# The places of three weight splits in the queues of VectorE and ScalarE, in a transformer block with a mixture of experts

## The chip, the cores and the metric

The kernel runs on one core of a Trainium2 chip, in float32 from HBM to HBM. The engines of the core are TensorE (PE, with its weight loads apart as PEld), VectorE (DVE), ScalarE (ACT), GpSimd (POOL) and SyncE (SP, which issues DMAs here). They work each through a queue of its own in order, and wait for each other by semaphores. The metric is the time of one execution in microseconds of the device. Three runs of the kernel before are there, and one profiled execution, from which all rows come. The granted clock of TensorE stands at one of its two levels, 1.2 or 2.4 GHz; its mean over the profiled execution was 0.864 of full speed.

## What is computed

The input is x, 32 sequences of 64 tokens with 256 features. Four layers follow one another:

```python
# 1: adapter: one of 16 domain experts for each sequence, then a layer norm
hidden = gelu(x @ down_W.T + down_b)
hidden = where(valid, hidden @ expert_W[idx].T + expert_b[idx], hidden) + domain_emb[idx]
x = layernorm(hidden @ up_W.T + up_b + x) * gamma + beta
# 2: attention with 16 heads of 16, a bias for each pair, a mask; feed-forward 256 -> 1024 -> 256
x = ln(x) * (1 + scale) + shift
probs = softmax(where(mask, -inf, q @ k.T / 4 + bias))
x = x + (probs @ v) @ Wo + bo
h = ln(x) * g2 + beta2
x = x + gelu2(h @ W1 + b1) @ W2 + b2
# 3: pairs of features rotated by theta and phi of the sequence
x = stack([x0*ct + x1*st, -x0*st + x1*ct, x2*cp + x3*sp, -x2*sp + x3*cp])
# 4: norm, norm over time, style, then a mixture of 8 experts, the best 2 for each token
h = ((ln(x)*g + b) normed over the tokens) * gamma3 + beta3
probs = softmax(h @ router)
y = sum over the best two experts e of gate_e * (relu(h @ w1[e] + b1[e]) @ w2[e] + b2[e])
return x + y
```

The expert weights of layer 4 (8 experts, two matrices of 256 x 1024 each) come as float32. The kernel multiplies the tokens with them as pairs of float16 halves: a high half, and the low half that the high one leaves over.

## The kernel before

**Stages.** The tokens are worked in NCH = 4 chunks of 512 (8 sequences). After a setup, chunk 0's layer 1 and 2 run; then a loop over c = 0, 1, 2 ("round c") holds on every engine, interleaved by hand, the second half of chunk c (feed-forward, rotation, norms, routing) with the attention of chunk c + 1 and the adapter of chunks c + 2 and c + 3. A tail ends the last chunk, a plan sorts the tokens by expert, and the experts' phase goes over 39 tiles of 128 rows from about 490 us to the end.

**Splits.** Beside all this, the expert weights are turned into halves and stored in HBM (`w_split`), to be loaded again for the experts' phase. There are 16 parts of 1 MB, numbered (c, q): chunk c = 0 to 3 carries parts q = 0 to 3, the two matrices of experts 2c and 2c + 1. All of them go through one tile `stage` and one tile `split`, so one part follows another:

- SP, `load_part(c, q)` (L430) waits until the low split of the part before is done, then issues the load into `stage`. `store_part(c, q)` (L437) waits for the low split of its part and issues the store from `split`. SP's queue holds store(c, q), then load(c, q + 1), and among them the loads of the attention's bias and of x.
- ACT, `split_high(c, q)` (L652): waits for the load and for the store of the part before, then writes the high half (L657).
- DVE, `split_low(c, q)` (L916): waits for the high half, then writes the low half (L920) and so frees `stage`.

**Order in a round.** It is written out by hand, in the loops at L779 (ACT), L1275 (DVE) and L1668 (PE). What stands where in round c matters:

- ACT: `feed_forward_in(c)` copies the transposed norm of PE to `h_f` (L707), `feed_forward(c, ...)` does the eight gelus (L713), split_high(c + 1, 0), exponentials, split_high(c + 1, 1), exponentials, queries and keys, `context`, `norm3(c)` (the copy L719), `context`, split_high(c + 1, 2), `token_gates`, `rows` (L731), and last `store(c)`, which waits for DVE's `accumulate` and issues the DMA of the chunk's output (L743). In rounds 1 and 2, split_high(c, 3) stands behind the fifth of the eight gelus; so it does for the last chunk, behind the loop.
- DVE: `values`, the adapter's residual and `norms` of chunk c + 2, split_low(c, 3) in rounds 1 and 2, `scores(0)` (additions L1033, maximum L1035), `scale_norm`, split_low(c + 1, 0), `scores(1)`, `sums(0)` (L1040, L1041), `rotate` (L1066 to L1078), `sums(1)`, `norm3` (statistics L953 to L948, and L963, which releases PE's transposes), split_low(c + 1, 1), `style` (L1091 to L1108), `residual`, the choice of experts, `fill_rows` (L1166), `norm2` of chunk c + 1 (the lines of norm3 again), `accumulate` (L1180), the adapter's `hidden` (L974), split_low(c + 1, 2).
- PE: `turn2(c)` (L1424), feed-forward (L1562, L1571) around the scores of chunk c + 1 (L1498), queries and keys (L1459), `context(c + 1, 0)` (L1516, L1526), `turn3(c)` (L1424), `context(c + 1, 1)`, output projection (L1542), routing, and the start of chunk c + 3.
- POOL: `residual`, mask of the biases (L517), the maxima subtracted (L536), the probabilities (L542), the odd half of the rotation (L560 to L563), and `dispatch(c)`, eight indirect DMAs (L573) that write the rows of the chunk to the place of their experts.

`split_low` in full, since it is what moves:

```python
def split_low(c, q):
    dve.wait_ge(split_hi.sem, split_hi.of(c, q + 1))
    part, high, low = split_of(q)
    dve.scalar_tensor_tensor(low, part, W_SCALE, high, ALU.mult, ALU.subtract).then_inc(split_lo.sem, 1)
```

## Time and profile before

| What | us |
|---|---|
| three runs: lowest, median, highest | 752.83, 753.59, 755.81 |
| the profiled execution: its own time | 752.83 |
| the profiled execution: span from first to last instruction | 751.0 |
| busy in the span: PE, DVE, ACT, POOL | 576.8, 484.2, 262.0, 271.4 |
| PE busy in round 0 (137 to 230), round 1 (230 to 330), round 2 (330 to 417) | 80.94, 77.45, 67.97 |
| DVE busy in the same stretches | 81.05, 78.51, 60.99 |
| start of PE's feed-forward (L1562) of chunks 1, 2 and 3 | 224.48, 324.86, 411.36 |
| end of the last weight store, and of the loads of the first five experts' weights | 431.85, 473.39 |

Busy time alone tells little here, since in the rounds neither PE nor DVE is busy throughout. The questions are which engine waits for which, and what stands in the queue behind a waiting instruction. The profile has four views for this. The chain of waits is followed back from the last instruction, at each step to what released it. The timeline of an engine gives each instruction with the idle time in front of it and what ended that. The groups of one tile gather all that reads or writes it. The DMA issues carry the time from issue to landing.

### The profile page before, as it was taken

To read this page: it belongs to the slowest core of one execution; us is meant where nothing else is said; L and a number is where in the kernel's file an instruction comes from. 1 tells how busy PE (TensorE), PEld (TensorE's weight loads), DVE (VectorE), ACT (ScalarE), POOL (GpSimd) and SP (SyncE) were. 2 spreads that over 40 slices of the span, in tenths; PEclk is the share of its full clock that TensorE was granted. 3 is DMA by queue.
4 is the path that set the end of the run, shared out by engine and by line. 5 is a ranking of instruction groups with operands and counts; after the bars stand their busy time and mean duration, and the time that the engine had idled before them with its cause. 6 is when DMAs were issued, how large, how long until landed. Compare 5 with 4: busy or idle time off the path is not lost.

```text
span 751.0 us, 16208 instructions
## 1 busy us (share of the span) xinstructions
PE 576.8 (77%) x5068; PEld 432.0 (58%) x5069; DVE 484.2 (64%) x1306; ACT 262.0 (35%) x548; POOL 271.4 (36%) x200
## 2 busy tenths in 40 slices
PE   3518587996979877769576963439999999999992
PEld 1416384583864756638474452327778777777771
DVE  5673785899789798626987136715656565656661
ACT  1215534425343253143332301004444444443440
POOL 0731728167055370327803220400323333323332
PEclk9559699999888999779885895559999999999997
DMA  8622473130325323174132567465222222222320
GB/s 287 231 81 78 147 254 140 36 114 0 113 99 211 134 92 113 44 266 166 59 113 78 175 238 261 181 242 168 48 43 47 42 43 39 42 45 34 49 42 1
DMA packets 41144, 86.28 MB, mean 115 GB/s; under 512 B 7317, under 2 KB 31790, under 8 KB 37006
## 3 DMA queue, kind: packets, MB, share of 16 engines
q1 hardware_dynamic: 22896, 65.13, 24.9%
q0 software_dynamic: 7200, 8.60, 6.7%
q10 hardware_dynamic: 11006, 12.01, 5.2%
q8 instruction: 25, 0.41, 0.2%
q14 instruction: 17, 0.14, 0.1%
HBM read 57.18 MB, written 29.44 MB: 115 GB/s over the span
## 4 chain that ended last, share of the span: by engine, by line
PE 49%; DVE 22%; issue 9%; DMA 7%; ACT 4%; ACTq 3%; POOL 3%; another core or an unknown queue 1%; POOLq 0%; SPq 0%; DVEq 0%
PE bank L1740 7%; PE bank L1562 6%; PE bank L1729 4%; PE bank L1731 4%; PE bank L1730 4%; DMA out_x<-x_kept,ids 4%; PE bank L1571 4%; PE bank L1741 3%; PE bank L1459 2%; DMA stage<-in_moe_w 2%; PE bank L1526 2%; PE bank L1542 2%; DVE stats L953 2%; PE bank L1516 2%; DVE w_moe L1076 2%
## 5 line engine op out<-in xcount | busy, mean ns | idle before, releaser
L1729 PE MATMUL bank<-xs_f,w_moe 128*128 128x128 f16 x624 | 123.9, 221 | 7.2 <-issue 5.7
L1731 PE MATMUL bank<-xs_f,w_moe 128*128 128x128 f16 x624 | 123.9, 221 | 0.0
L1730 PE MATMUL bank<-xs_f,w_moe 128*128 128x128 f16 x624 | 123.4, 221 | 0.0
L831 ACT ACTIVATE stage<-bank,cols 128x128 f32<-128x128 f32 x312 | 88.6, 376 | 95.6 <-PE bank L1731 82.9
L1729 PEld LDWEIGHTS bank<-xs_f,w_moe 128*128 x624 | 61.4, 98 | 43.1 <-issue 14.4
L629 POOL DMA_INDIRECT out_x<-x_kept,ids x39 | 62.0, 1590 | 64.4 <-DVE x_kept L1379 34.4
L1740 PE MATMUL bank<-w_moe,split 128*128 x208 | 78.6, 380 | 0.9
L573 POOL DMA_INDIRECT dispatched<-disp,slot x32 | 34.6, 1080 | 119.4 <-DVE disp L1166 55.6
L1562 PE MATMUL bank<-w_moe 128*128 128x512 f32 x128 | 63.0, 655 | 9.9 <-ACT w_moe L707 9.9
L1730 PEld LDWEIGHTS bank<-xs_f,w_moe 128*128 x624 | 61.6, 99 | 2.6
L920 DVE SCALAR_TENSOR_TENSOR split<-stage,split 128x2048 f16<-128x2048 f32 x16 | 39.9, 2494 | 35.2 <-ACT split L657 35.2
L1731 PEld LDWEIGHTS bank<-xs_f,w_moe 128*128 x624 | 61.4, 98 | 0.9
L1571 PE MATMUL bank<-w,w_moe 128*128 128x256 f32 x256 | 58.3, 387 | 0.8 <-ACT w_moe L713 0.8
L1741 PE MATMUL bank<-w_moe,split 128*128 x208 | 56.7, 273 | 0.0
L625 POOL COPY ids<-meta 128x1 uint32 (+1 forms) x39 | 13.2, 339 | 117.4 <-DMA out_x<-x_kept,ids 100.8
L657 ACT ACTIVATE split<-stage 128x2048 f16<-128x2048 f32 x16 | 30.5, 1906 | 69.9 <-DMA stage<-in_moe_w 53.4
L1571 PEld LDWEIGHTS bank<-w,w_moe 128*128 128x128 f32 x256 | 49.1, 194 | 9.0 <-ACT w_moe L713 1.6
L536 POOL TENSOR_TENSOR w_moe<-w_moe,sc_max 128x2048 f32<-128x2048 f32 x8 | 30.9, 3868 | 62.0 <-DVE sc_max L1035 62.0
L1424 PE MATMUL bank<-mats,w_moe 128*128 128x128 f32 x96 | 17.7, 345 | 45.8 <-DVE w_moe L963 45.6
L1562 PEld LDWEIGHTS bank<-w_moe 128*128 128x128 f32 x128 | 26.7, 212 | 44.2 <-issue 31.8
L517 POOL TENSOR_TENSOR w_moe<-w_moe,mask_add 128x512 f32<-128x512 f32 x32 | 41.5, 1334 | 21.6 <-DMA w_moe<-in_bias 21.5
L1364 DVE COPY xs_f<-bank 128x512 f16<-128x512 f16 x40 | 16.9, 424 | 48.1 <-PE bank L1719 48.1
(242 smaller groups left out, 1248.1 us busy)
## 6 DMA issues: line engine op xcount, KB each, us to landing
stage<-in_moe_w SPq DMA_DIRECT2D x16, 1024.0 KB, 8.4
w_split<-split SPq DMA_DIRECT2D x16, 1024.0 KB, 4.9
w_moe<-w_split SPq DMA_DIRECT2D x8, 2048.0 KB, 8.1
w_moe<-in_bias SPq DMA_DIRECT2D x8, 1024.0 KB, 10.5
xs<-dispatched ACTq DMA_DIRECT2D x41, 130.0 KB
w_moe<-in_x_f SPq DMA_DIRECT2D x4, 512.0 KB, 5.8
w_moe<-in_x_t SPq DMA_DIRECT2D x4, 512.0 KB, 5.0
out_x<-x4b ACTq DMA_DIRECT2D x4, 512.0 KB
```

The costliest lines, as they stand in the source:

```text
L517: pool.tensor_tensor(sc[u][:, r], sc[u][:, r], mask_add[:, bass.ds(c * TT + 2 * u, 2), :].unsqueeze(2).broadcast_to([P, 2, 4, S]), ALU.add ...
L573: pool.indirect_dma_start(out=xs_dram[:, :], out_offset=bass.IndirectOffsetOnAxis(ap=slot[:, a, i:i + 1], axis=0), in_=disp[:, i, :], in_o ...
L629: pool.indirect_dma_start(out=out[:, :], out_offset=bass.IndirectOffsetOnAxis(ap=ids[j][:, 0:1], axis=0), in_=ys[j], in_offset=None, bound ...
L831: ins = act.activation(h32[j][:, f, :], bank[2 * j + g][:, P * (f % 4):P * (f % 4) + P], ACT.Relu, bias=moe_b1[:, bass.ds(e, 1), f], scale ...
L920: dve.scalar_tensor_tensor(low, part, W_SCALE, high, ALU.mult, ALU.subtract).then_inc(split_lo.sem, 1)
L1562: mm = pe.matmul(bank[4 + f % 2][:], w1[:, k, P * f:P * f + P], h_f[:, k, :], start=(k == 0), stop=(k == KD - 1))
L1571: mm = pe.matmul(bank[6 + i // 2][:, D * (i % 2):D * (i % 2) + D], ff[:, f, P * i:P * i + P], w2[:, f, :], start=(f == 0), stop=(f == KF - 1))
L1729: pe.matmul(o, hi, xs_f[j][:, k, :], start=(k == 0), stop=False)
L1730: pe.matmul(o, hi, xs_f[j][:, KD + k, :], start=False, stop=False)
L1731: mm = pe.matmul(o, lo, xs_f[j][:, k, :], start=False, stop=(k == KD - 1))
L1740: pe.matmul(o, h_hi[m][:, f, :], rows_of, start=(f == 0), stop=(f == KF - 1), skip_group_check=True)
L1741: mm = pe.matmul(o[:, 0:D], h_lo[m][:, f, :], rows_of[:, 0:D], start=False, stop=(f == KF - 1), skip_group_check=True)
```

## The change

The splits of parts 1, 2 and 3 of a chunk move to other places in the queues of DVE and ACT. On DVE, split_low(c + 1, 1) stands in front of `norm3` instead of behind it; split_low(c + 1, 2) stands in front of `norm2` instead of at the end of the round; split_low(c + 1, 3) stands at the end of round c, instead of in front of `scores(0)` of the next round (for the last chunk: it stays in front of the tail). On ACT, split_high(c + 1, 3) stands in front of `store(c)` instead of between the gelus of the next round's feed-forward. The code of SP, PE and POOL is untouched; SP's waits for the splits are met at other times. No instruction is added or taken away, and the same values are computed.

```diff
@@ ACT, loop over the rounds
             for c in range(NCH - 1):
                 feed_forward_in(c)
-                if c > 0:
-                    feed_forward(c, range(5))
-                    split_high(c, 3)
-                    feed_forward(c, range(5, KF))
-                else:
-                    feed_forward(c, range(KF))
+                feed_forward(c, range(KF))
                 split_high(c + 1, 0)
...
                     keep(c + 2)
                     values(c + 2)
+                split_high(c + 1, 3)
                 store(c)
             feed_forward_in(NCH - 1)
-            feed_forward(NCH - 1, range(5))
-            split_high(NCH - 1, 3)
-            feed_forward(NCH - 1, range(5, KF))
+            feed_forward(NCH - 1, range(KF))
@@ DVE, loop over the rounds
                     norms()
-                if c > 0:
-                    split_low(c, 3)
                 scores(0)
...
                 sums(1)
+                split_low(c + 1, 1)
                 norm3()
-                split_low(c + 1, 1)
                 style()
...
                 fill_rows()
+                split_low(c + 1, 2)
                 norm2()
                 accumulate()
                 if c + 3 < NCH:
                     hidden, adapter_residual, norms = adapter(c + 3)
                     hidden()
-                split_low(c + 1, 2)
-            split_low(NCH - 1, 3)
+                split_low(c + 1, 3)
```

ACT's queue at the end of round 2 and the feed-forward of the last chunk; L657 is the high split, L743 the issue of the output's DMA, L707 the copy, L713 the gelus:

```order
 L731 ACTIVATE disp<-bank 128x2x256 x2
+L657 ACTIVATE split<-stage 128x8x256
 L743 DMA out_x<-x4b 128x4x256
 L707 ACTIVATE w_moe<-bank,cols 128x512 x2
 L713 ACT_TABLE_LOAD
-L713 ACTIVATE w_moe<-bank,cols 128x512 x5
-L657 ACTIVATE split<-stage 128x8x256
-L713 ACTIVATE w_moe<-bank,cols 128x512 x3
+L713 ACTIVATE w_moe<-bank,cols 128x512 x8
```

The high split of part 3 has moved from between the gelus to a place in front of the output's DMA and of the copy.

DVE's queue at the end of round 2, before; L1166 is `fill_rows`, L953 to L963 `norm2`, L1180 `accumulate`, L920 the low split:

```order
L1166 TENSOR_TENSOR disp<-bank,disp 128x2x256 x2
L953 BN_STATS stats<-w_moe 128x6 x4
...
L963 TENSOR_SCALAR w_moe<-w_moe,mv,rstd 128x256 x4
L1180 TENSOR_TENSOR x4b<-bank,w_moe 128x512 x2
L920 SCALAR_TENSOR_TENSOR split<-stage,split 128x2048
L920 SCALAR_TENSOR_TENSOR split<-stage,split 128x8x256
L1066 TENSOR_TENSOR w_moe<-bank,w_moe 128x512 x2
```

The same place in the changed kernel, where the lines of these functions are six lower (the low split is L914):

```order
L1160 TENSOR_TENSOR disp<-bank,disp 128x2x256 x2
L914 SCALAR_TENSOR_TENSOR split<-stage,split 128x2048
L947 BN_STATS stats<-w_moe 128x6 x4
...
L957 TENSOR_SCALAR w_moe<-w_moe,mv,rstd 128x256 x4
L1174 TENSOR_TENSOR x4b<-bank,w_moe 128x512 x2
L914 SCALAR_TENSOR_TENSOR split<-stage,split 128x8x256
L1060 TENSOR_TENSOR w_moe<-bank,w_moe 128x512 x2
```

The low split of part 2 now stands in front of the statistics of norm2; that of part 3 keeps its place in front of the last chunk's rotation, but its wait is for a high split that stands elsewhere on ACT.

DVE's queue around norm3 of round 2, before; L1040 and L1041 are `sums(1)`, L953 to L963 norm3, L1091 the start of `style`:

```order
L1040 TENSOR_REDUCE sc_sum<-w_moe 128x32
L1041 RECIPROCAL sc_inv<-sc_sum 128x32
L953 BN_STATS stats<-w_moe 128x6 x4
...
L963 TENSOR_SCALAR w_moe<-w_moe,mv,rstd 128x256 x4
L920 SCALAR_TENSOR_TENSOR split<-stage,split 128x8x256
L1091 BN_STATS stats<-h 128x6 x16
```

And in the changed kernel:

```order
L1034 TENSOR_REDUCE sc_sum<-w_moe 128x32
L1035 RECIPROCAL sc_inv<-sc_sum 128x32
L914 SCALAR_TENSOR_TENSOR split<-stage,split 128x8x256
L947 BN_STATS stats<-w_moe 128x6 x4
...
L957 TENSOR_SCALAR w_moe<-w_moe,mv,rstd 128x256 x4
L1085 BN_STATS stats<-h 128x6 x16
```

The low split of part 1 has moved from between norm3 and `style` to a place between the sums and norm3.

## Rows read from the trace of the kernel before

**Rows 1.** Chain of waits, whole program: start us, us, what stood in it.
```profile
248.46 8.43 DMA stage<-in_moe_w
256.91 1.92 ACT split L657
...
340.86 8.30 DMA stage<-in_moe_w
...
398.94 10.49 issue
409.43 0.38 ACTq L743
409.86 1.46 ACT w_moe L707 x2
```

**Rows 2.** Tile `stage`: durations ns min/median/max, first and last start; last its loads.
```profile
L657 ACT ACTIVATE split<-stage x16: 1893/1910/1911, 40.5 to 423.7; 128x2048 f16<-128x2048 f32 x16
L920 DVE SCALAR_TENSOR_TENSOR split<-stage,split x16: 2228/2284/4733, 51.0 to 425.7; 128x2048 f16<-128x2048 f32 x16
...
DMA to landing us min/median/max: 5.8/8.4/9.4
```

**Rows 3.** Timeline of DVE: start us, us, engine, line, what [idle before <-releaser].
```profile
258.85 2.29 DVE L920 SCALAR_TENSOR_TENSOR split<-stage,split 128x2048 f16<-128x2048 f32 x1 [4.89 <-ACT split L657]
...
351.12 2.31 DVE L920 SCALAR_TENSOR_TENSOR split<-stage,split 128x2048 f16<-128x2048 f32 x1 [4.56 <-ACT split L657]
```

**Rows 4.** Timelines of DVE, POOL and PE around norm3 of round 0, same columns.
```profile
178.49 1.34 DVE L953 BATCH_NORM_STATS2 stats<-w_moe 128x6 f32<-128x256 f32 x4
...
187.75 2.28 DVE L920 SCALAR_TENSOR_TENSOR split<-stage,split 128x2048 f16<-128x2048 f32 x1
189.96 2.11 DVE L1091 BATCH_NORM_STATS2 stats<-h 128x6 f32<-128x64 f32 x16
...
178.65 3.62 POOL L542 TENSOR_TENSOR w_moe<-w_moe,sc_inv 128x2048 f32<-128x2048 f32 x1 [1.64 <-DVE sc_inv L1041]
...
187.89 1.97 PE L1424 MATMUL bank<-mats,w_moe 128*128 128x128 f32 x8 [5.87 <-DVE w_moe L963]
```

**Rows 5.** Timelines of DVE and POOL where a split meets POOL, early chunks.
```profile
92.06 2.23 DVE L920 SCALAR_TENSOR_TENSOR split<-stage,split 128x2048 f16<-128x2048 f32 x1
...
155.69 4.73 DVE L920 SCALAR_TENSOR_TENSOR split<-stage,split 128x2048 f16<-128x2048 f32 x1
...
92.22 5.54 POOL L542 TENSOR_TENSOR w_moe<-w_moe,sc_inv 128x2048 f32<-128x2048 f32 x1 [0.42 <-DVE sc_inv L1041]
```

**Rows 6.** Timelines of DVE and SP at the end of round 2.
```profile
401.79 1.27 DVE L1166 TENSOR_TENSOR disp<-bank,disp 128x512 f16<-128x512 f32 x2
...
409.32 2.27 DVE L920 SCALAR_TENSOR_TENSOR split<-stage,split 128x2048 f16<-128x2048 f32 x1
...
412.01 0.43 SPq L433 DMA_DIRECT2D stage<-in_moe_w  x1
```

**Rows 7.** Timelines of DVE, ACT and PE at the ends of rounds 0 and 1.
```profile
210.25 1.27 DVE L1166 TENSOR_TENSOR disp<-bank,disp 128x512 f16<-128x512 f32 x2
...
307.85 1.27 DVE L1166 TENSOR_TENSOR disp<-bank,disp 128x512 f16<-128x512 f32 x2
...
321.60 1.29 DVE L1180 TENSOR_TENSOR x4b<-bank,w_moe 128x512 f32<-128x512 f32 x2 [7.34 <-remote]
...
221.62 1.51 ACT L707 ACTIVATE w_moe<-bank,cols 128x512 f32<-128x512 f32 x2 [8.49 <-remote]
...
224.48 16.40 PE L1562 MATMUL bank<-w_moe 128*128 128x512 f32 x32
```

**Rows 8.** Timelines of PE, DVE and POOL in round 2.
```profile
350.27 2.66 PE L1498 MATMUL bank<-w_moe 32*64 32x128 f32 x64
...
353.36 2.47 DVE L1033 TENSOR_TENSOR w_moe<-bank,w_moe 128x512 f32<-128x512 f32 x4
...
361.81 3.62 POOL L542 TENSOR_TENSOR w_moe<-w_moe,sc_inv 128x2048 f32<-128x2048 f32 x1
```

## The prediction

> **What bounds the kernel now.** I read the chain of waits first, then the groups of the tile `stage`, then the timelines of DVE, ACT, PE, POOL and of SP's DMA issues around each place where a split stands. "Round c" is one pass of the loop over c = 0, 1, 2 (about 137 to 230, 230 to 330 and 330 to 417 us); "split(c, q)" is part q of chunk c, with its high half on ACT (L657) and its low half on DVE (L920).
>
> The chain of the first 500 us runs over all engines in turn, with no engine that bounds it alone. Two of its pieces are waits for a part of the expert weights: in rounds 1 and 2 the load of part (c+1, 0) and the high split behind it stand in the chain with 8.43 + 1.92 us and again with 8.30 us. At the end of round 2 it waits on ACT, whose next work, the copy that feeds feed-forward of the last chunk, starts at 409.86 [rows 1]. A low split costs DVE 2.28 us in the median, a high split costs ACT 1.91, and a load lands 8.4 us after its issue, 5.8 at best and 9.4 at worst [rows 2]. What the two waits of the chain cost is less than 10 us each, because other work goes on below them: DVE idled 4.89 and 4.56 us in front of the low split (c+1, 0) [rows 3]. These two are what the change can win; 9.5 us is the most.
>
> **Part 1: split (c+1, 1) in front of norm3, three times.** Before, this split stood behind norm3 and was free. In round 0 norm3 released the transposes on PE at 187.89, after PE had idled 5.87 us for them; `style` on DVE could not start before ACT had copied their result, and began at 189.96. The split filled just this gap, 187.75 to 190.03 [rows 4]. In front of norm3 it delays norm3, the transposes, the context products and output projection queued behind them on PE, and `style`, and the gap behind norm3 stays open. Cost 2.2 us in each of three rounds, since the row of the statistics at 178.49 follows the softmax sums without idle time. Bounds: 0, if norm3 had to wait for POOL's half of the rotation anyway, and the stretched form below.
>
> Here DVE and POOL also meet. The rows show that a low split and a tensor operation of POOL exclude one another: with the split first, POOL's multiplication took 5.54 us where it takes 3.62; with POOL first, the split took 4.73 where it takes 2.28 [rows 4, 5]. In the new place POOL's multiplication by the inverse sums is released by the same DVE instruction that the split follows; in the pattern of 92.06 the split started first, by 0.16 us, so I take 2.2 for DVE and shift POOL. The small operations of norm3 wait for POOL then as they do now, only later.
>
> The Trainium skill, SBUF — State Buffer, section "SBUF: two separate sides", says that VectorE and GpSimd share one port pair under an exclusive lock, which the instruction that starts first keeps to its end; the trace agrees (5.54 and 4.73). What follows if POOL comes first is rival 2.
>
> **Part 2: split (c+1, 2) in front of norm2, and split (c+1, 3) at the end of the round.** The load of part 3 is issued only when the low split of part 2 is done, since both use the one `stage` tile. On ACT the high split of part 3 now stands in front of `store` and of the copy that feeds feed-forward. ACT works in order, so feed-forward of the next chunk waits for: low split 2, issue, load, high split, issue of the store. Before, none of these stood there.
>
> End of round 2, first with no shift from earlier. `fill_rows` ends at 401.79 + 1.27 = 403.06 [rows 6]. Low split 2.28: 405.34. From a low split's end (409.32 + 2.27 = 411.59) to the issue of the load at 412.01 it takes 0.42 [rows 6]: 405.76. Load 8.4: 414.16. High split 1.91 and 0.02 to start it: 416.09. The store's issue, by the gap from 409.43 to 409.86 [rows 1], 0.43: 416.52. The copy started at 409.86, so this boundary costs **6.7 us**. The 2.28 us for norm2 and the accumulation lie inside it: they would end near 411.6. PE's feed-forward, queued behind the copy, moves by the same 6.7. The landing sets the bounds: 5.8 gives 4.1, 9.4 gives 7.7.
>
> By the Trainium skill, DMA: Bandwidth & Descriptors, section "Anatomy of one DMA — SWDGE (gpsimd) path", a transfer costs about 2.0 us and its bytes over 436 GB/s; for 1 MiB that is an estimate of 4.4 us, with which the boundary would cost 2.7. The rows of this kernel, with 1 MB out and 1 MB in queued together, show 8.4, and they decide.
>
> End of round 0, shifted by 2.2 from part 1: `fill_rows` ended at 210.25 + 1.27 = 211.52 [rows 7]. 211.52 + 2.2 + 2.28 + 0.42 + 8.4 + 1.93 + 0.43 = 227.2 for a copy that started at 221.62: 5.6 us later. PE's feed-forward began at 224.48, behind another wait, and the copy takes 1.5, so it begins near 228.7, 4.2 later. DVE has its own split(1, 3) near 226.8 to 229.0 and is some 6 us late for the norms of chunk 3.
>
> End of round 1: `fill_rows` ended at 307.85 + 1.27 = 309.12, and with the shift of 0.8 derived below the high split would be done near 323.0. Before, DVE stood still for 7.34 us until 321.60 in front of the accumulation, a wait whose cause the profile doesn't name (PE's result came late) [rows 7]; the copy came behind it. If this wait is still there, the splits hide in it, and the boundary costs only what it is shifted, 0.8.
>
> **Part 3: what comes back.** In round 1 the delay of 4 to 6 us meets the wait that is gone. Split(1, 3) no longer stands in front of the scores (2.2 us), load (2, 0) is long landed (4.89 us of idling gone), and the masks of POOL, whose bias load no longer stands behind a late weight load, slow fewer of DVE's norms (about 3 us). But DVE is then next held by POOL (low split (2, 0) behind the subtraction of the maxima, as in the row of 4.73) and by PE, which is 3 us late with its scores. My estimate from these pieces is that the second maximum of the scores comes 1.4 us early. Part 1 takes 2.2 again: round 1 hands on +0.8.
>
> In round 2 PE's last scores were done at 350.27 + 2.66 = 352.93, while DVE's additions ran to 353.36 + 2.47 = 355.83, late by the wait for split (3, 0). Without it they end 0.7 behind PE: 352.93 + 0.8 + 0.7 = 354.4, 1.4 early; the POOL multiplication at 361.81, which holds up the rotation, moves with them [rows 8]. With part 1's 2.2: +0.8 at `fill_rows`. So of the 9.5 us nearly all goes to repay the boundaries and part 1, and the last boundary, behind which no weight wait is left to remove, is paid in full.
>
> **Sum.** 0.8 + 6.7 = 7.5 us. Nothing behind it gives this back: the weights were loaded long before the experts began, and the experts' phase shifts as a whole. The profiled execution took 752.83 us (its span 751.0), so 752.83 + 7.5 = 760.3; it is the fastest of the three runs, whose median is 753.59, and against that the sum is 761.1. I give **761.0**.
>
> **Rivals.**
> Rival 1, the delays add up: the norms of chunk 3 gain nothing from the earlier masks (3 us), and rounds 1 and 2 hand on +3.7 instead of +0.8. Then 753.6 + 3.7 + 6.7 = 764.0. For it: the DVE and POOL rows depend on which comes first by tenths of a microsecond. Against: round 2 has slack of its own on PE.
> Rival 2, POOL first at the lock in front of norm3: the split takes up to 2.28 + 3.62, of which 1.8 comes back because norm3's first small operation no longer waits; some 1.8 more per round, and not all of it survives to the end: about 763.
> Rival 3, a shorter load: at the last boundary the queue is emptier, the load lands in 5.8 us, or the rounds before gain 3 us more: 761.1 - 2.6 to 761.1 - 5.6, about 757.
> Rival 4, not slower: the ends of the rounds hide their loads and the removed waits count in full: 753.6 - 4.89 - 4.56 + 3 x 2.2 = 750.7. For it: DVE's 7.34 us at the end of round 1 show that such a hole exists. Against: at the end of round 2 there is none; it decides from the point at which the load needs under 8.4 - 6.7 = 1.7 us there, or round 2 reaches `fill_rows` 6.7 us early, and no row shows a load under 5.8.
> Rival 5, the change does nothing, since the order of two queues is unlike what I read: 753.6. The listings of the new order speak against it.
>
> **How the numbers follow.** Forecast 0.57, rival 1 0.17, rival 2 0.10, rival 3 0.10, rival 4 0.04, rival 5 0.02. Range: 756.5 to 765.0 holds the forecast with both bounds of the load (758.5 to 762.1), rivals 1 and 2 and most of rival 3. A change of 0.5%, 3.8 us, is about what can be told from none. Under 749.8 lies a part of rival 4, 0.02; within 749.8 to 757.4 the rest of it, rival 5 and about half of rival 3, 0.10; above, 0.88.
>
> **What would show it.** Right: in the last round ACT idles some 7 us before the high split that stands in front of the store, for the load, and the copy L707 starts near 417 instead of 409.86; DVE no longer idles 4.9 and 4.6 us before split (c+1, 0); DVE has an idle gap of about 2 us behind norm3, waiting for L719; the high split of part 3 of round 1 hardly moves the copy. Wrong: a load in the last round that landed before accumulation, or a start of the statistics of norm3 in round 2 that is over 3 us early or late.

## The result, and the profile after

The changed kernel takes 760.9 us in the median of five runs (759.66 to 762.53) beside 753.44 for the kernel before on the same chip: a ratio of 1.0097 (95% interval 1.0083 to 1.0112). The forecast was 761.0. In a second run of its own the change stood at 1.0103 (1.0075 to 1.0131; last experiment). The profiled execution of after took 761.58 us, its span is 759.8 against 751.0.

Line numbers of after are lower than those of before: DVE's by 6 (the split is L914), PE's by 8 (the transposes are L1416, the feed-forward L1554); those of ACT, POOL and SP are the same.

The tile `stage`, as in [rows 2], first. The columns are shortest, median and longest duration in ns, then first and last start:

```profile
L657 ACT ACTIVATE split<-stage x16: 1893/1909/1912, 40.4 to 416.9; 128x2048 f16<-128x2048 f32 x16
L914 DVE SCALAR_TENSOR_TENSOR split<-stage,split x16: 2228/2282/4736, 51.1 to 418.9; 128x2048 f16<-128x2048 f32 x16
```

The same work takes the same time; what changed is who waits. The chain of waits of after (start, length, what) has lost both loads of a part (c + 1, 0) that [rows 1] showed, and has three others, one at the end of each round:

```profile
215.63 9.41 DMA stage<-in_moe_w
...
312.91 9.44 DMA stage<-in_moe_w
...
407.64 9.25 DMA stage<-in_moe_w
```

The last of them in full, from the timelines of DVE, SP, ACT and PE in after (start, duration, what, and in brackets the idle time in front with its releaser):

```profile
403.77 1.27 DVE L1160 TENSOR_TENSOR disp<-bank,disp 128x512 f16<-128x512 f32 x2
404.96 2.27 DVE L914 SCALAR_TENSOR_TENSOR split<-stage,split 128x2048 f16<-128x2048 f32 x1
407.64 0.43 SPq L433 DMA_DIRECT2D stage<-in_moe_w  x1
412.27 1.28 DVE L1174 TENSOR_TENSOR x4b<-bank,w_moe 128x512 f32<-128x512 f32 x2
416.92 1.91 ACT L657 ACTIVATE split<-stage 128x2048 f16<-128x2048 f32 x1 [15.99 <-DMA stage<-in_moe_w]
416.92 0.38 ACTq L743 DMA_DIRECT2D out_x<-x4b  x1
418.73 1.43 ACT L707 ACTIVATE w_moe<-bank,cols 128x512 f32<-128x512 f32 x2
420.22 2.08 PE L1554 MATMUL bank<-w_moe 128*128 128x512 f32 x2 [5.84 <-ACT w_moe L707]
```

DVE's accumulation ends at 413.55, so the store and the copy L707 could go then. They go at 416.92 and 418.73, because the high split stands ahead of them on ACT and its load landed 9.25 us after the issue. Against [rows 6] and [rows 1], `fill_rows` is 1.98 us late (403.77 for 401.79) and the copy 8.87 (418.73 for 409.86): this one boundary makes 6.9 us.

The place of norm3 in round 0, answering [rows 4], on DVE, POOL and PE of after:

```profile
177.61 2.23 DVE L914 SCALAR_TENSOR_TENSOR split<-stage,split 128x2048 f16<-128x2048 f32 x1
177.77 5.53 POOL L542 TENSOR_TENSOR w_moe<-w_moe,sc_inv 128x2048 f32<-128x2048 f32 x1 [1.66 <-DVE sc_inv L1035]
188.93 1.97 PE L1416 MATMUL bank<-mats,w_moe 128*128 128x128 f32 x8 [7.80 <-DVE w_moe L957]
190.89 2.12 DVE L1085 BATCH_NORM_STATS2 stats<-h 128x6 f32<-128x64 f32 x16 [2.02 <-ACT h L719]
```

DVE comes first at the lock (by 0.16 us), POOL's multiplication stretches to 5.53 us, PE idles 7.80 us instead of 5.87, and the gap of 2.02 us in front of `style`, which the split used to fill, is open. All three rounds show the same.

**A ledger of starts.** The start of an execution varies: the first copy L707, up to which the code is the same in all kernels (but for the place of one bias load in e12), stood between 131.88 and 135.62 us in the profiles of this study. So I compare places by their distance from that first copy, called the mark below. An entry is this distance in a kernel less the same distance in before. For after the first copy is at 131.88 (before: 132.78), `style` of round 0 at 190.89 (before: 189.96), so the entry is 59.01 - 57.18 = +1.83. The columns are, for the rounds 0, 1 and 2: the start of `style`; the start of the copy L707 at the end of that round; and max1 and max2, the start of POOL's second subtraction of a maximum (L536) in rounds 1 and 2.

```
                           style0  copy0  max1  style1  copy1  max2  style2  copy2
change                      +1.8   +6.3   -0.6   +1.2   +1.9   +0.7   +2.5   +9.8
change once more            +1.8   +6.1   -0.6   +1.2   +1.5   +0.5   +2.3   +9.3
```

Round 0 ends 6.3 late and gets it all back until the middle of round 1; the end of round 1 costs little (1.2 to 1.9); each norm3 costs 1.8; the last boundary is paid and stays.

### The profile page after: what moved, and what is told of

It is laid out like the page before. It is cut to its first block, busy times and chain, and to the rows that moved or that the text cites. A ratio compares the mean times of both kernels' runs of the same rounds, so it can differ in the third digit from the quotient of the medians.

```text
span 759.8 us, 16208 instructions
## 1 busy us (share of the span) xinstructions
PE 577.8 (76%) x5068; PEld 433.1 (57%) x5069; DVE 481.5 (63%) x1306; ACT 262.7 (35%) x548; POOL 281.6 (37%) x200
## 3 DMA queue, kind: packets, MB, share of 16 engines
HBM read 57.18 MB, written 29.44 MB: 114 GB/s over the span
## 4 chain that ended last, share of the span: by engine, by line
PE 55%; DVE 21%; DMA 8%; issue 5%; ACT 3%; POOL 3%; ACTq 3%; POOLq 0%; SPq 0%; DVEq 0%
PE bank L1563 8%; PE bank L1732 7%; PE bank L1554 6%; PE bank L1721 4%; PE bank L1723 4%; PE bank L1722 4%; DMA out_x<-x_kept,ids 4%; DMA stage<-in_moe_w 4%; PE bank L1733 3%; PE bank L1451 2%; PE bank L1518 2%; PE bank L1534 2%; PE bank L1508 2%; DVE split L914 2%; PE bank L1490 2%
## 5 line engine op out<-in xcount | busy, mean ns | idle before, releaser
L1554 PE MATMUL bank<-w_moe 128*128 128x512 f32 x128 | 63.1, 656 | 16.2 <-ACT w_moe L707 16.2
L1416 PE MATMUL bank<-mats,w_moe 128*128 128x128 f32 x96 | 19.9, 375 | 57.2 <-DVE w_moe L957 57.2
L536 POOL TENSOR_TENSOR w_moe<-w_moe,sc_max 128x2048 f32<-128x2048 f32 x8 | 32.9, 4114 | 72.8 <-DVE sc_max L1029 72.8
L1554 PEld LDWEIGHTS bank<-w_moe 128*128 128x128 f32 x128 | 26.8, 212 | 50.7 <-issue 33.2
L657 ACT ACTIVATE split<-stage 128x2048 f16<-128x2048 f32 x16 | 30.5, 1907 | 70.9 <-DMA stage<-in_moe_w 54.6
L914 DVE SCALAR_TENSOR_TENSOR split<-stage,split 128x2048 f16<-128x2048 f32 x16 | 42.9, 2681 | 15.6 <-ACT split L657 15.6
L1416 PEld LDWEIGHTS bank<-mats,w_moe 128*128 128x128 f32 x96 | 15.9, 194 | 60.5 <-DVE w_moe L957 58.0
```

Source lines behind the costliest of these rows:

```text
L1416: mm = pe.transpose(bank[first_bank + k][:, P * i:P * i + P], z[:, i, P * k:P * k + P], ident[:])
L1554: mm = pe.matmul(bank[4 + f % 2][:], w1[:, k, P * f:P * f + P], h_f[:, k, :], start=(k == 0), stop=(k == KD - 1))
```

## The experiments

Each ratio is to runs of the kernel before on the same chip. The experiments did not all have the same chip: the kernel before took 753.1 us in the median beside e1 to e4, 753.5 beside e5, e6, e8 and e9, 747.0 beside e10 to e12, and 754.2 beside e13. The ledger of all of them:

```
                           style0  copy0  max1  style1  copy1  max2  style2  copy2   ratio
e1  split 1 back             0.0   +3.9   -3.4   -3.4   -2.1   -3.0   -3.0   +3.1   1.0044
e2  split 1 alone           +1.8   +5.2   +6.6   +8.4   +5.7   +6.7   +8.5   +7.5   1.0154
e3  last high split back    +1.8   +6.1   -0.5   +1.2   +1.6   +0.6   +2.4   +5.1   1.0064
e4  last boundary alone      0.0   -1.5   -0.4   -0.4   -1.5   +0.1   +0.1   +6.7   1.0084
e5  rounds 0 and 1 only      0.0   +4.3   -3.3   -3.3   -1.9   -2.9   -2.9   -3.0   0.9950
e6  low 2 in residual        0.0   -0.8   -1.6   -1.6   -1.9   -2.9   -2.9   -3.1   0.9962
e8  the same, norm3 late    +1.8   +5.3   +5.5   +7.3   +8.1   +7.3   +9.1   +9.7   1.0102
e9  half the last load      +1.8   +6.8   -0.4   +1.4   +1.7   +0.7   +2.5   +6.7   1.0087
e10 split 1, round 0        +1.8   -0.3   +0.9   +0.9   -5.4   -4.4   -4.4   -4.0   1.0022
e11 split 1, round 2         0.0   -3.2   -0.4   -0.4   -7.5   -6.7   -4.8   -4.2   1.0031
e12 low 2 in residual, bias later
                             0.0   -3.2   -4.4   -4.4   -9.6  -11.8  -11.8  -12.9   0.9912
```

e4 runs before's code up to the end of round 2, and its entries up to max2 lie between -1.5 and +0.1: that is how well the ledger repeats. e10 to e12 have another chip under them and are read against each other (e11 is before's code up to max2).

The ledger is of one execution each, the ratios are of several. At copy2 the two agree within 1 us for e1, e3 to e6 and e9. They don't for the change and e8, where the ledger has 9.3 to 9.8 and the ratios 7.3 to 7.8 us, and not for e2, where the ledger has 7.5 and the ratio 11.6. So wherever a kernel is set against the change, the ledger shows some 2 us more than the timed runs.

### What split 1 in front of norm3 costs

```diff
--- change
+++ e1
-                split_low(c + 1, 1)
                 norm3()
+                split_low(c + 1, 1)
```

> The change, but with split_low(c+1,1) behind norm3 again, as in the kernel before; the other moves stay. Theory (the split in front of norm3 costs about 2 us in a round, and a weight wait removed behind it gives part of that back in rounds 0 and 1): in the last round style starts 1.8 to 2.2 us earlier against fill_rows' predecessor, and the end comes 2 to 4 us earlier than the change: 757 to 759 us, 1.004 to 1.007 of the kernel before. Rival (the moved split only fills idle time that opens elsewhere, all of the loss is the late split (c+1,3)): within 0.7 us of the change, 760 to 761.6. Rival 2 of the prediction (POOL first at the lock) would show POOL's multiplication at 3.62 us and the split at 4.7 in front of norm3.

Measured: 756.76 us, 1.0044 (1.0020 to 1.0069). That is 0.0053 to 0.0059 less than the change, 4.0 to 4.4 us, where 2 to 4 were expected; in the ledger it is 6.2 to 6.7. There one also sees each norm3 giving 1.8 back; in round 1 `style` is 4.6 us ahead of the change's. The rival with no effect fell.

The other way round, the same move alone on the kernel before:

```diff
--- before
+++ e2
-                norm3()
                 split_low(c + 1, 1)
+                norm3()
```

> The kernel before, with only split_low(c+1,1) moved in front of norm3. Theory: about 2 us later in the last round, plus what rounds 0 and 1 hand on: 755.5 to 759.5 us, likeliest 757.5. Rival (the move is free because something else is late): within 0.7 us of the kernel before. POOL's multiplication by the inverse sums should take 5.5 us instead of 3.6 in all three rounds.

Measured: 763.82 us, 1.0154 (1.0130 to 1.0179). That is 11.6 us by the ratio and 10.7 between the medians, far over the expectation, and more than the whole change costs. The three steps at `style` are 1.8 us again (0 to 1.8, 6.6 to 8.4, 6.7 to 8.5), so the rest comes between them. In round 0 the ledger goes from 1.8 to 5.2. Two things are seen there, in the timelines of PE, DVE and ACT of e2:

```profile
215.17 5.40 PE L1477 MATMUL bank<-w_moe 128*64 128x128 f32 x64 [0.45 <-DVE slot L1143]
229.61 0.68 DVE L974 TENSOR_TENSOR w_moe<-bank,add_o 64x512 f32<-64x512 f32 x1 [2.93 <-remote]
229.67 1.45 ACT L707 ACTIVATE w_moe<-bank,cols 128x512 f32<-128x512 f32 x2 [9.63 <-remote]
```

PE's 64 matmuls of the values took 5.40 us; before they took 3.74. In the change it is 5.40 too. The values of round 0 in before, then in after:

```profile
209.89 3.74 PE L1477 MATMUL bank<-w_moe 128*64 128x128 f32 x64 [0.45 <-DVE slot L1143]
```

```profile
211.38 5.40 PE L1469 MATMUL bank<-w_moe 128*64 128x128 f32 x64 [0.45 <-DVE slot L1137]
```

The windows of both kernels show the granted clock (PEclk, third number from the end, as a share of full speed) at the upper of its two levels all through in before, and at the lower for part of the stretch in after; first before, then after:

```profile
209.00:215.00 6.00, 5.55 (x75) 4.91 (x74) 5.55 (x24) 3.42 (x5) 1.81 (x2) 1.00 0.07 24
```

```profile
209.00:215.00 6.00, 5.25 (x50) 4.85 (x51) 5.72 (x18) 3.72 (x5) 0.61 (x1) 0.72 0.01 3
```

What preceded it is PE's idle time of 7.8 us instead of 5.9 at norm3. The two go together in all fourteen traces: the seven with the split in front of norm3 in round 0 have 7.8 and 5.40, the other seven 5.9 and 3.73 to 3.74. And then DVE and ACT wait for results of PE that come late without the profile naming a cause ("remote"), as in the 7.34 us of [rows 7]. In the change both are hidden, since the load of part 3 is what its ACT waits for at that time.

To see what one round's move costs by itself, I made it in round 0 alone and in round 2 alone:

```diff
--- before
+++ e10 (e11: 2 for 0)
+                if c == 0:
+                    split_low(c + 1, 1)
                 norm3()
-                split_low(c + 1, 1)
+                if c != 0:
+                    split_low(c + 1, 1)
```

> The kernel before, with split_low(c+1,1) in front of norm3 in round 0 alone. Theory (the 1.8 us at norm3 are multiplied in this round: PE idles 7.8 us instead of 5.9, its clock falls once more, its values take 5.1 to 5.4 us instead of 3.7, and the end of the round stands about 5 us later): the second maximum of round 1 is 5 to 6.5 us late against a common mark, the hole at the end of round 1 takes 2 to 3 of it, and the kernel takes 756 to 758.5 us. Rival (a price of 1.8 to 2.4 us in each round, handed on as it is): 754.5 to 756.

> The kernel before, with split_low(c+1,1) in front of norm3 in the last round (round 2) alone. Theory (1.8 us at norm3 and about 0.5 at the residual, nothing behind gives it back): style 1.8 us late, the last copy L707 2.2 to 2.6 us late, 755.5 to 756.2 us. Rival (most of the 10.7 us of the run with all three is made here): over 758.

Measured: e10 748.00 us beside 746.95, 1.0022 (1.0007 to 1.0038), 1.7 us. e11 748.97 us, 1.0031 (1.0016 to 1.0045), 2.3 us. The absolute times expected were for a before of 753.1 and don't hold. As differences, e11's theory was right (2.4 to 3.1 told; in its ledger -6.7 to -4.8 at `style`, another 0.6 until the copy), and e10's 2.9 to 5.4 was too much, although PE idled 7.80 us there too and its values took 5.40: its rival, a price of about 2 us handed on as it is, came near. Against e11, e10's ledger is 2.9 late at copy0, 1.4 at max1 and 2.1 to 2.3 from copy1 on. So a norm3 delayed by the split costs 1.7 and 2.3 us in rounds 0 and 2 (by the intervals 0.5 to 2.8 and 1.2 to 3.4). Thrice that is some 6 us, near the 7.5 of e2's own ledger, and the 11.6 of e2's timed runs stay partly unexplained: on the chip of e10 no result of PE came late, on that of e2 they did, and no run repeats e2 on another chip.

### What the last boundary costs

```diff
--- change
+++ e3 (ACT)
+                if c + 2 < NCH:
+                    split_high(c + 1, 3)
-                split_high(c + 1, 3)
                 store(c)
             feed_forward_in(NCH - 1)
-            feed_forward(NCH - 1, range(KF))
+            feed_forward(NCH - 1, range(5))
+            split_high(NCH - 1, 3)
+            feed_forward(NCH - 1, range(5, KF))
```

> The change, but the high half of the very last part, split (3,3), stands between the gelus of the last feed-forward again, as in the kernel before; all of DVE's order and rounds 0 and 1 stay as changed. Theory (ACT's copy waits for the load of part 3, and nothing behind gives it back): the copy L707 starts near 412 plus the store's 0.4 us and ends the boundary with about 2.3 us left of 6.9 (low split 2 still stands in front of norm2): 4.5 us less than the change, 755.5 to 757.5. Rival 1 (the delay is a loss of order elsewhere, the boundary only moves): 759.5 to 761.5. Rival 2 (feed-forward then waits at the sixth gelu for the late high split): no gain over 2 us.

Measured: 758.62 us, 1.0064 (1.0043 to 1.0085), 2.5 to 3 us less than the change's ratios give, where 4.5 were expected. The trace has the mechanism as told. The timelines of DVE and ACT of e3:

```profile
408.62 2.27 DVE L917 SCALAR_TENSOR_TENSOR split<-stage,split 128x2048 f16<-128x2048 f32 x1
415.93 1.28 DVE L1177 TENSOR_TENSOR x4b<-bank,w_moe 128x512 f32<-128x512 f32 x2
417.67 1.45 ACT L707 ACTIVATE w_moe<-bank,cols 128x512 f32<-128x512 f32 x2 [13.10 <-DVE x4b L1177]
```

The copy waits for the accumulation and no longer for the load; by the ledger the boundary is 5.1 - 2.4 = 2.7 us, of which 2.3 is the low split in front of norm2, and copy2 is 4.2 to 4.7 earlier than in the change. The timed gain is outside the expectation and 1.5 us under that of the trace. That is the difference that the ledger shows for everything set against the change (some 2 us); where it comes from is open. Rival 2 fell: the late high split stood behind the fifth gelu, at 430.73, 19 us after the issue of its load, and started without idle time.

```diff
--- before
+++ e4
                 fill_rows()
+                if c + 2 == NCH:
+                    split_low(c + 1, 2)
                 norm2()
...
+                if c + 2 == NCH:
+                    split_high(c + 1, 3)
                 store(c)
```

(and the later places of both taken away for that round.)

> The kernel before, with only the end of the last round changed: split_low(3,2) in front of norm2 and split_high(3,3) in front of the store; rounds 0 and 1 and the order around norm3 as before. Theory: this boundary alone makes 6.7 to 7.1 us, so 760.1 to 760.6 us; rounds 0 and 1 and the moves at norm3 then balance to less than 1 us in the change. Rival (the boundary's cost is only large because the load meets the shifted dispatch traffic): the load lands in 6 to 8 us and the kernel takes 757 to 759.

Measured: 759.65 us, 1.0084 (1.0064 to 1.0105), 6.5 us more than the 753.11 of its own before (6.3 by the ratio). The rival fell: the load was issued at 406.06 and ended at 415.15, 9.1 us, as long without the shift. So the last boundary alone makes 6.3 to 6.5 of the change's 7.3 to 7.8 us. Its other moves cost about 1 us together by the timed runs, which is inside the intervals, and 2.5 to 3 by the ledger.

Is it the length of the load? In e9 the very last load is halved (the second half of that part's weights is then not its own data):

```diff
--- change
+++ e9
                 w_part = t["moe_w1"] if q % 2 == 0 else t["moe_w2"]
+                if c == NCH - 1 and q == 3:
+                    sp.dma_start(stage[:].rearrange("p (k n) -> p k n", k=KF)[:, 0:KF // 2, :],
+                                 w_part[bass.ds(c * 2 + q // 2, 1), 0:P * KF // 2, :].rearrange("e (k p) n -> p (e k) n", p=P)
+                                 ).then_inc(stage_in.sem, 16)
+                    return
```

> The change, with only half of the last part (3,3) loaded, so that half of that part's weights is not computed from its own data. Theory (the time of the load stands in the chain): the load lands in 5 to 7 us instead of 9.3, and the kernel gains as much as the landing comes earlier, 2.5 to 4 us: 757 to 758.5 us. Rival (the store of part 2, which is queued ahead and must have ended before the high split, sets the start): under 1.5 us gained.

Measured: 760.15 us, 1.0087 (1.0069 to 1.0104). SP's and ACT's timelines of e9:

```profile
409.94 0.43 SPq L434 DMA_DIRECT2D stage<-in_moe_w  x1
416.02 1.91 ACT L662 ACTIVATE split<-stage 128x2048 f16<-128x2048 f32 x1 [12.81 <-DMA stage<-in_moe_w]
417.84 1.43 ACT L712 ACTIVATE w_moe<-bank,cols 128x512 f32<-128x512 f32 x2
```

From the issue to the start of the high split it is 6.08 us for half the bytes, instead of 9.28 (the chain of waits has the load itself at 5.82, instead of 9.25), and the boundary shrinks with it in the ledger: 6.7 - 2.5 = 4.2 instead of 7.3. The timed gain, 0.8 to 1.2 us by the ratios, is smaller than the 2.5 expected, lies inside the intervals, and is what the rival gave (under 1.5). The rival's reason is not what the traces have: in after the store of part 2, issued at 407.26, landed after 5.13 us, 4.5 us before the load, and the high split started 0.03 us behind its load there and 0.26 in e9. So the trace says that the load is in the chain; the timed runs did not confirm the size.

Half the bytes for 3.2 to 3.4 us less means some 2.4 to 3 us fixed and 6.4 to 6.9 for 1 MiB, an estimate of 150 to 165 GB/s from 6.08 or 5.82 and 9.25. The Trainium skill, DMA: Bandwidth & Descriptors, section "Anatomy of one DMA — SWDGE (gpsimd) path", has about 2.0 us fixed and 436 GB/s for a DMA that GpSimd issues. For this load, which SP issues, the fixed part is near and the rate isn't, with a store of 1 MiB and the rows of `dispatch` under way at the same time.

### What the change has to give

```diff
--- e1
+++ e5
-                split_low(c + 1, 2)
+                if c + 2 < NCH:
+                    split_low(c + 1, 2)
                 norm2()
...
+                if c + 2 == NCH:
+                    split_low(c + 1, 2)
                 split_low(c + 1, 3)
```

(and ACT as in e3.)

> The change without its two costly parts: split_low(c+1,1) behind norm3 again, and the last round's parts 2 and 3 handled as in the kernel before; only rounds 0 and 1 keep split 2 in front of norm2 and split 3 at the end of the round. Theory (the removed waits are worth about 3 us at the last fill_rows, by the trace of e1_split1_back against a common mark, and nothing is paid back): 749.5 to 751.5 us, 0.995 to 0.998 of the kernel before. Rival (the early state only lets another wait grow in the last round): 752.4 to 754.

Measured: 750.11 us, 0.9950 (0.9934 to 0.9965), inside the expectation. Without the moves at norm3 and at the last boundary, what is left is a gain of 3.4 to 3.8 us: the removed waits of [rows 3], less what the ends of rounds 0 and 1 cost.

Next, the load could be issued earlier, so that it is in nobody's way. DVE idles 1.9 us between the two additions of `residual()`; e6 puts the low split of part 2 there:

```diff
--- e1
+++ e6
                     for g in range(2):
+                        if g and between:
+                            between()
                         dve.wait_ge(wo_done.sem, wo_done.of(c, g + 1))
...
-                residual()
+                residual(lambda: split_low(c + 1, 2))
...
-                split_low(c + 1, 2)
                 norm2()
```

> split_low(c+1,1) behind norm3 again, and split_low(c+1,2) between the two additions of residual(), where DVE idles 1.9 us; split_high and split_low of part 3 as in the change. Theory (all that the boundary costs is that the load of part 3 is issued too late): load 3 is issued 9 us earlier and lands in front of the accumulation, the copy L707 waits for no load in any round, each residual pays 0.3 to 0.7 us, and the kernel takes 745 to 750 us, likeliest 748. Rival (the load's cost comes back because the high split of part 3 or the dispatch traffic still stands before the copy, or PE is the bound once DVE is early): 750 to 753.

> The change with one move more: split_low(c+1,2) stands between the two additions of residual() and not in front of norm2; split_low(c+1,1) stays in front of norm3. Theory: the 6.9 us of the last boundary go, those of norm3 (1.8 us a round) stay: 7 to 9 us less than the change, 751 to 754 us. Rival (the boundary's delay is not the load's): 758 to 761.

Measured: e6 750.63 us, 0.9962 (0.9945 to 0.9979), less than hoped and in the rival's range. e8, the same move made on the change with norm3 still late: 761.61 us, 1.0102 (1.0084 to 1.0120), no gain at all, as the rival had it. But its reason was another. At the last boundary the theory held: the ledger goes from 9.1 at style2 to 9.7 at copy2, 0.6 us where the change pays 7.3. What was won there had been lost in round 0: e8 stands at +5.5 at max1, where the change stands at -0.6. The timelines of DVE and POOL of e8:

```profile
229.32 12.24 DVE L914 SCALAR_TENSOR_TENSOR split<-stage,split 128x2048 f16<-128x2048 f32 x1
229.59 9.82 POOL L517 TENSOR_TENSOR w_moe<-w_moe,mask_add 128x512 f32<-128x512 f32 x8
```

and of e6:

```profile
228.60 9.82 POOL L517 TENSOR_TENSOR w_moe<-w_moe,mask_add 128x512 f32<-128x512 f32 x8
228.77 9.68 DVE L933 TENSOR_SCALAR var<-mv 128x4 f32<-128x4 f32 x1
```

With load 3 issued earlier, the load of the attention's bias, which is queued behind it on SP, comes earlier too (issued at 205.76 in e6, 224.27 in before). POOL then finds its bias there and goes into its eight masks straight from the instruction in front of them. One instruction of DVE, whichever it is, stands until all eight are over: 12.24 us for a split of 2.28, 9.68 for a step of 0.17, and again 12.12 and 12.18 for the split of part 3 in round 1.

That the masks follow one another without idle time is not the reason, since they do so in every trace. In before POOL had waited 7.90 us for its bias in front of them, and DVE's small steps alternated with the masks and took 1.19 us each. In e11 the split stood for one mask only, although it came 0.1 us behind the first of the eight. DVE and POOL of e11:

```profile
329.36 3.32 DVE L920 SCALAR_TENSOR_TENSOR split<-stage,split 128x2048 f16<-128x2048 f32 x1 [10.35 <-ACT split L657]
329.26 11.89 POOL L517 TENSOR_TENSOR w_moe<-w_moe,mask_add 128x512 f32<-128x512 f32 x8 [5.83 <-DMA w_moe<-in_bias]
```

So what goes with the long block in these traces is that POOL came to the masks without waiting.

So e12 sends the bias later:

```diff
--- e6
+++ e12 (SP)
-                load_bias(c + 1)
                 store_part(c, 3)
                 load_part(c + 1, 0)
+                load_bias(c + 1)
```

> e6_low2_in_residual with one move more: the load of the score bias is queued behind the loads of part 3 and part (c+1,0), so that POOL's masks do not start while DVE stands in front of the low split of part 3. Theory (POOL's eight masks, run without a wait between them, shut DVE out: 9.7 and 12.2 us for one instruction): the low splits of part 3 take 2.3 us again, xn1 of chunk 3 is done about 2 us earlier, and the kernel takes 747.5 to 749.5 us. Rival (the masks cost DVE the same wherever they stand, or the scores now wait for them): 750 to 752.

Measured: 740.87 us beside 746.95, a ratio of 0.9912 (0.9893 to 0.9932), 6.1 to 6.6 us faster than the kernel before. This version beats both. (By ratio, the 747.5 to 749.5 expected beside 753.5 were 0.992 to 0.995.) The timelines of e12, DVE and POOL:

```profile
220.52 2.27 DVE L914 SCALAR_TENSOR_TENSOR split<-stage,split 128x2048 f16<-128x2048 f32 x1
235.44 9.84 POOL L517 TENSOR_TENSOR w_moe<-w_moe,mask_add 128x512 f32<-128x512 f32 x8 [5.62 <-DMA w_moe<-in_bias]
236.81 1.14 DVE L933 TENSOR_SCALAR var<-mv 128x4 f32<-128x4 f32 x1
237.98 1.20 DVE L934 TENSOR_SCALAR rstd<-var 128x4 int32<-128x4 int32 x1
245.72 1.38 DVE L957 TENSOR_SCALAR w_moe<-w_moe,mv,rstd 128x256 f32<-128x256 f32 x4
```

POOL waits for its bias again, and the same step L933 that stood for 9.68 us in e6 takes 1.14 beside the same eight masks. The low splits of part 3 take 2.27 and 2.28 us. Against e11, which is before's order on the same chip, the ledger is 3.9 us ahead at max1 (e6 against before: 1.6) and 5.1 at max2. How much of the gain over e6 is the bias and how much the chip isn't separated in round 1; in round 0 it is some 2 us for the bias, as expected. e6 was not run on this chip, nor e12 on the other.

### The hole at the end of round 1

Beside e10 to e12 the kernel before was 6.5 us faster than on the other chips. e11's timeline of DVE there, against the 7.34 us of [rows 7]:

```profile
314.00 1.49 DVE L1180 TENSOR_TENSOR x4b<-bank,w_moe 128x512 f32<-128x512 f32 x2 [0.41 <-PE bank L1619]
```

No late result, and copy1 is 7.5 us early in the ledger. So I ran the change itself again:

> The change itself, word for word, once more, to see how it stands where the kernel before takes 747 us and not 753. In the runs with a before of 747 us PE's result at the end of round 1 came in time (no idle time of 7 us in front of the accumulation), and the change's own trace has no such late result either. Theory (the difference of 6.5 us between these befores is that hole, and the change never had it): if the before of this run takes about 747, the change still takes 759 to 762 us, 1.016 to 1.020 of it; if the before takes about 753, the ratio is 1.008 to 1.011 again. Rival (those runs are faster all over): 753 to 756 beside a before of 747, a ratio of 1.008 to 1.011 in either case.

Measured: 762.59 us beside 754.16, 1.0103 (1.0075 to 1.0131). The chip it ran on was of the slower kind for before, so the run repeats the result but does not tell the theory from its rival. Whether the change loses more where the hole is missing isn't known.

## Why the prediction was right, point by point

**Part 1, 2.2 us in each round.** Right in kind and near in size. In round 0 DVE was first at the lock by 0.16 us, POOL took 5.53, PE idled, and `style` waited 2.02 us for ACT. The step at `style` is 1.8 in all three rounds, not 2.2, since the small operations of norm3 wait a little less for POOL; another 0.4 to 0.6 comes until the residual, where the matmuls behind the longer idle time run at the lower clock. Timed one by one: 1.7 and 2.3 us. Rival 2, POOL first, did not occur.

**Part 2, the last boundary, 6.7 us.** Right: 6.9 in the trace of after, 6.5 timed alone (e4). Two terms were off and nearly cancelled: the load took 9.25 us and not 8.4, and the 0.43 us for the store's issue were not paid, since ACT's queue issued it beside the running split (both start at 416.92).

**Part 2, the end of round 0, copy L707 at 227.2.** It started at 227.00, PE's feed-forward at 228.50 (told: 228.7), from a start of the execution that was 0.9 us earlier; against the mark the copy is 6.3 us late (6.1 in e13) where 5.6 were told.

**Part 2, the end of round 1, hidden but for 0.8.** The copy started at 324.31, 0.95 later than before. The condition was that the unexplained wait be still there. It was not: in after DVE's accumulation goes without idle time, and ACT waits for the load in its place.

```profile
317.53 1.28 DVE L1174 TENSOR_TENSOR x4b<-bank,w_moe 128x512 f32<-128x512 f32 x2
322.37 1.91 ACT L657 ACTIVATE split<-stage 128x2048 f16<-128x2048 f32 x1 [9.75 <-DMA stage<-in_moe_w]
324.31 1.45 ACT L707 ACTIVATE w_moe<-bank,cols 128x512 f32<-128x512 f32 x2
```

(DVE and ACT of after.) A load takes up as much time as the hole did, and so the number came near by luck: 0.95 between the two traces, 1.9 against the mark (1.5 in e13), for 0.8. That the hole goes when the load comes is seen also in e1, e3, e5 and e9, where the low split of part 2 stands in front of norm2 in round 1, and not in e2, e4, e6 and e8, where it doesn't; why, isn't shown.

**Part 3, round 1 gives back until the second maximum is 1.4 us early.** The subtraction behind it started at 264.44 for 265.94, 1.5 early. But 0.9 of that is the earlier start of the execution; against the mark it is 0.6 early, in both traces of the change. So the way was right, and the gain was told 0.8 us too large. Split (2, 0) met POOL's subtraction at the lock and took 4.74 us, as told.

**Part 3, round 2 gives back until 1.4 us early.** This is the step that was most mis-sized. PE and POOL of after:

```profile
325.81 16.50 PE L1554 MATMUL bank<-w_moe 128*128 128x512 f32 x32 [6.17 <-ACT w_moe L707]
351.93 2.66 PE L1490 MATMUL bank<-w_moe 32*64 32x128 f32 x64
358.00 3.62 POOL L536 TENSOR_TENSOR w_moe<-w_moe,sc_max 128x2048 f32<-128x2048 f32 x1 [4.10 <-DVE sc_max L1029]
```

and PE of before, for the first of them:

```profile
324.86 15.79 PE L1562 MATMUL bank<-w_moe 128*128 128x512 f32 x32 [8.78 <-ACT w_moe L707]
```

The subtraction stood at 358.23 before, so only 0.2 us were won, and against the mark it is 0.7 late (0.5 in e13). The prediction took PE's scores as shifted by the 0.8 us of the boundary; they are 1.66 late (351.93 for 350.27, [rows 8]), of which 0.95 is the copy and 0.7 is feed-forward at a lower clock, and DVE's additions end 1.0 behind PE's scores instead of 0.7. So round 2 handed on 2.0 us at `fill_rows` instead of 0.8, and 2.9 against the mark.

**The sum.** Told: 0.8 + 6.7 = 7.5 between the profiled executions, 761.0 for the median. The two profiled executions differ by 8.75 us, and the copy by 8.87, which is 2.0 + 6.9; against the mark it is 9.8 late (9.3 in e13). The medians differ by 7.46, and by 8.4 in e13; all twenty executions of after have a median of 761.3. So the exact hit is partly luck: the traces bear out a sum 1.2 to 2.3 us larger than the one told, and the timed runs one that is up to 0.9 larger. **Rival 1**, 764, had the mis-sized step in it: 2.9 us more handed on by rounds 1 and 2, where the traces show 1.2, and 2.1 against the mark. **Rival 4**, the gain in full, is refuted by e4 at the last boundary and has a true core, shown by e5: in rounds 0 and 1 the removed waits are worth more than the ends of the rounds cost. **Rival 3**'s shorter load did not occur.

## What to carry to other kernels

Where a load, the work that frees its buffer and the work that uses it are moved together, follow the whole loop (free, issue, land, use) to the first instruction that is queued behind the use on an in-order engine, and do it at the last round by itself: what earlier rounds pay can come back, what the last pays doesn't. Look for the early release of the buffer inside idle time that is there anyway (here 1.9 us between two additions) rather than in front of something that others wait for. And when a transfer moves, follow what is queued behind it: here the bias load of POOL, two places further, brought one instruction of DVE to stand for 10 us. The order that avoided it gained 6 us where the other gained 3, though on another chip, so that how much of this is the bias isn't shown.

## What the runs showed of the hardware

- The Trainium skill, SBUF — State Buffer, section "SBUF: two separate sides", has the lock held for one whole instruction. In e6 and e8 it was not handed over between back-to-back instructions of POOL: one DVE instruction stood for all eight masks, 12.24 us for a split of 2.28 and 9.68 for a step of 0.17. Elsewhere, as in e5 behind 234.9 us, DVE's small steps alternate with masks and take 1.19 each. In the four long blocks POOL had no idle time in front of the masks; in the rounds of the other kernels it had waited 0.5 to 13.6 us for its bias. Why that should decide isn't shown.
- POOL's issue of an indirect DMA is held up too while a low split runs: the first of `dispatch` took 2.21 us in after (at 405.91, with the split from 404.96 to 407.23) and 1.00 in before, where the sixth took 2.12 (at 410.31, with the split from 409.32 to 411.59). The Trainium skill, SBUF — State Buffer, section "SBUF: two separate sides", says that GpSimd can't write the descriptors of its own DMAs while VectorE runs an operation in a two-port mode. Of an operation with two inputs, like the low split, it says only that it contends with a GpSimd operation that reads SBUF. The traces show the delay for the low split (2.21 and 2.12); by which of these ways it comes, no run shows.
- Results of PE reached DVE and ACT up to 6.5 us after the recorded end of the matmuls (315.06 to 321.60 in before), at the ends of rounds 0 and 1, in some runs and in some orders only. On the chip where they were missing the kernel before took 747 us and not 753. The cause is open.
- The longer idle time of PE in front of the transposes of norm3 in round 0 (7.8 us for 5.9) was followed by a stretch at a lower granted clock (0.72 for 1.00 between 209 and 215 us), and the 64 matmuls of the values took 5.40 us instead of 3.74.
